# Splitting the last stage's first part into halves, with the last block's squares summed on VectorE and a pile of six blocks

## What is computed

```
def _gn(v, G=16, eps=1e-05):            # mean and variance over H, W and pairs of channels
    g = v.reshape(B_, H_, W_, G, C_ // G)
    return ((g - m) / jnp.sqrt(s + eps)).reshape(v.shape)

def _L3_conv_ref(x, weight, idx_a, idx_b):
    cross = x[..., idx_a] * x[..., idx_b]          # all 496 pairs of a row
    feat = jnp.concatenate([x, x * x, cross], axis=-1)
    return jnp.einsum('bcij,cijo->bcio', feat, weight)

x = x + _L3_conv_ref(_gn(x), ...)
```

## Time and profile before

| | us |
|---|---|
| median of 3 runs | 809.18 |
| lowest and highest run | 802.34, 817.39 |
| the profiled execution | 816.41 |
| its span in the profile | 814.5 |
| the seam's first small reduction to the first gather | 507.10 to 526.56 |

### The profile page before, as it was taken

One profiled execution on the slowest core, in us unless ns is written; L12 is line 12 of the kernel. 1 busy time (PEld: TensorE's weight loads), 2 busy tenths in 40 slices (PEclk: granted clock), 3 DMA queues, 4 the chain that ended last, 5 costly groups with the idle time before them and its releaser, 6 DMA issues.

```text
span 814.5 us, 57339 instructions
## 1 busy us (share of the span) xinstructions
PE 522.6 (64%) x26570; PEld 402.6 (49%) x26570; DVE 576.1 (71%) x698; ACT 435.8 (54%) x724; POOL 294.2 (36%) x412
## 2 busy tenths in 40 slices
PE   0036665326699999437665257167887868878786
PEld 0025555326588878236655222045655546555554
DVE  4989999899543432699989896446765747767563
ACT  5229999491121221359999362235655645656452
POOL 1049884000555520089882021431414224141110
PEclk9996999858799999857889569589998989999897
DMA  8809999400399999439999200458999899999990
GB/s 342 369 11 349 397 397 399 178 0 1 125 319 347 403 402 405 191 109 391 395 397 362 76 1 0 124 157 306 306 380 348 275 332 314 383 357 325 344 340 24
DMA packets 49846, 217.56 MB, mean 267 GB/s; under 512 B 7552, under 2 KB 17792, under 8 KB 29312
## 3 DMA queue, kind: packets, MB, share of 16 engines
q1 hardware_dynamic: 40336, 210.06, 69.7%
q10 hardware_dynamic: 9216, 6.30, 2.5%
q0 software_dynamic: 240, 0.53, 0.2%
HBM read 202.18 MB, written 8.39 MB: 259 GB/s over the span
## 4 chain that ended last, share of the span: by engine, by line
PE 31%; DVE 27%; DMA 17%; issue 9%; POOL 9%; ACT 5%; ACTq 1%; SPq 0%; DVEq 0%; POOLq 0%
PE psum L836 12%; DMA wring<-in_own 9%; DVE stats L631 5%; PE psum L946 5%; PE psum L919 5%; POOL xn_ring L254 4%; PE psum L930 4%; DVE abs_sums L699 3%; DMA wring<-in_w 3%; DMA beyond<-state_b 2%; ACT state_b L598 2%; DVE state_b L799 2%; DVE xn_ring L254 2%; POOL state_a L374 2%; POOL near L385 2%
## 5 line engine op out<-in xcount | busy, mean ns | idle before, releaser
L799 DVE TENSOR_TENSOR state_b<-psum,state_b 128x512 f32<-128x512 f32 x256 | 164.9, 685 | 110.2 <-ACT state_b L598 109.9
L598 ACT ACTIVATE state_b<-psum 128x512 f32<-128x512 f32 x256 | 140.6, 594 | 118.0 <-PE psum L919 114.6
L836 PE MATMUL psum<-signs,near 64*32 64x96 f16 (+3 forms) x6528 | 128.2, 220 | 98.7 <-DMA beyond<-nothing 36.8
L836 PEld LDWEIGHTS psum<-signs,near 64*32 64x32 f16 (+1 forms) x6528 | 115.1, 104 | 107.7 <-issue 107.2
L699 DVE TENSOR_REDUCE abs_sums<-wring 128x1 f32<-128x2048 f32 x64 | 142.9, 2276 | 0.1
L474 ACT ACTIVATE signs<-wring 128x2304 f16<-128x2304 f32 x64 | 134.8, 2107 | 0.0
L946 PE MATMUL psum<-state_b,wring 128*32 128x32 f32 x8192 | 109.5, 204 | 29.0 <-issue 12.0
L946 PEld LDWEIGHTS psum<-state_b,wring 128*32 128x32 f32 x8192 | 90.6, 116 | 67.8 <-issue 30.5
L919 PE MATMUL psum<-signs,sel 64*128 64x512 f16 x512 | 90.9, 409 | 44.4 <-POOL signs L408 19.6
L836 PE MATMUL psum<-wring,near 64*32 64x96 f32 (+5 forms) x3264 | 96.5, 241 | 16.4 <-DMA beyond<-nothing 10.6
L836 PEld LDWEIGHTS psum<-wring,near 64*32 64x32 f32 (+1 forms) x3264 | 86.9, 108 | 23.9 <-issue 23.9
(11 more groups left out here) (141 smaller groups left out, 797.6 us busy)
## 6 DMA issues: line engine op xcount, KB each, us to landing
wring<-in_w SPq DMA_DIRECT2D x96, 1152.0 KB, 10.2
wring<-in_pairs SPq DMA_DIRECT2D x64, 1024.0 KB, 9.2
wring<-in_own SPq DMA_DIRECT2D x32, 256.0 KB, 9.3
wring<-split SPq DMA_DIRECT2D x32, 256.0 KB, 5.3
state_a<-in_x SPq DMA_DIRECT2D x8, 512.0 KB, 9.3
split<-signs SPq DMA_DIRECT2D x8, 512.0 KB, 8.0
out<-state_a SPq DMA_DIRECT2D x32, 128.0 KB, 9.0
beyond<-state_b ACTq DMA_DIRECT2D x112, 32.0 KB, 5.9
```

Of the source, the lines that this page charges most:

```text
L598: act.activation(left[:, n % LSLOTS, :], psum[:, n % ASLOTS, :], ACT.Copy, scale=1.0 / HALF_SCALE / HALF_SCALE).then_inc(left_made, 1)
L799: dve.tensor_tensor(feats[:, n % FSLOTS, :], psum[:, ASLOTS + n % BSLOTS, :], left[:, n % LSLOTS, :], ALU.mult).then_inc(feats_made, 1)
L836: last = pe.matmul(psum[g * B:(g + 1) * B, bank, (a * C) % 512:(a * C) % 512 + (b - a) * C], acts[q, j, s, k, :], weights[q, j, kind, s, ( ...
```

## The change

Three edits. First, the statistics: the pile has six blocks (GpSimd makes five additions) and TensorE takes it right after the sums of block 6; block 7's squares are reduced by VectorE to 32 columns, and TensorE passes these 32 columns through the same matrix into bank 6; VectorE adds the two 32-column results. Second, part 0 is normalised, split into high and low, written to DRAM and read back in two halves of 512 columns, each with semaphores of its own; the first ring copies wait for the first half only. SyncE's queue holds put and get of the first half, put and get of the second, then those of part 1. Third, GpSimd starts part 1 only when the low half of all of part 0 is made.

```diff
--- before.py
+++ after.py
@@ -62,7 +62,8 @@
 FSLOTS = 8
 LSLOTS = 3
 TILES = NK * PT
-PILED = 5
+PILED = 6
+PHALF = PART // 2
 
 
 def build(nc, x, w_conv, bias, gamma_beta, w_pairs, w_own, mats, sel_rows, sel_index, split, out):
@@ -174,11 +175,16 @@
         root = sem("root")
         dve_chain = sem("dve_chain")
         transposed = sem("transposed")
+        half_made = sem("half_made")
+        hi_half = sem("hi_half")
+        lo_half = sem("lo_half")
         part_made = sem("part_made")
         part_centred = sem("part_centred")
         hi_split = sem("hi_split")
         lo_split = sem("lo_split")
         squared = sem("squared")
+        half_out = sem("half_out")
+        half_in = sem("half_in")
         split_out = sems("split_out", V)
         parts_in = sems("parts_in", V)
         ring_made = sem("ring_made")
@@ -322,9 +328,21 @@
                         sp.dma_start(parts[first:first + W, i % 2, :, :],
                                      split[i, k].rearrange("(g w) n -> w g n", g=G)).then_inc(parts_in[i], 16)
 
-            for i in range(2):
-                put_split(i)
-                get_parts(i)
+            for half in range(2):
+                cols = slice(half * PHALF, (half + 1) * PHALF)
+                sp.wait_ge((hi_half, hi_split)[half], 1)
+                sp.wait_ge((lo_half, lo_split)[half], 1)
+                sp.dma_start(split[0][:, :, cols].rearrange("k p n -> p k n"), hi_lo[:, 0, :, cols]
+                             ).then_inc((half_out, split_out[0])[half], 16)
+                sp.wait_ge((half_out, split_out[0])[half], 16)
+                for side in range(2):
+                    for k in range(2):
+                        first = (2 * side + k) * W
+                        sp.dma_start(parts[first:first + W, 0, :, cols],
+                                     split[0, k][:, cols].rearrange("(g w) n -> w g n", g=G)
+                                     ).then_inc((half_in, parts_in[0])[half], 16)
+            put_split(1)
+            get_parts(1)
             for k in range(NK):
 
                 sp.wait_ge(mixed, PT * (k + 1))
@@ -402,7 +420,9 @@
             def copy_ring(k):
 
                 if k % (2 * GROUP) == 0:
-                    pool.wait_ge(parts_in[k // GROUP // 2], 16 * 2 * 2)
+                    pool.wait_ge(parts_in[k // GROUP // 2] if k else half_in, 16 * 2 * 2)
+                if k == GROUP:
+                    pool.wait_ge(parts_in[0], 16 * 2 * 2)
                 if k >= GROUP:
                     pool.wait_ge(gathered, (k - GROUP + 1) * PT)
                 pool.tensor_copy(ring[:, k % GROUP, :].rearrange("p (g n) -> p g n", g=G),
@@ -436,6 +456,7 @@
                 pool.tensor_tensor(dst, dst, r_op, ALU.mult).then_inc(part_made, 1)
 
             pool.wait_ge(part_made, 1)
+            pool.wait_ge(lo_split, 1)
             normalise_part(1)
             for grp in range(NGROUP):
                 copy_ring(grp * GROUP)
@@ -583,7 +604,10 @@
                 act.activation(own_xsq, xn[:, grp // 2 % 2, grp % 2 * GCOLS:(grp % 2 + 1) * GCOLS],
                                ACT.Square).then_inc(squared, 1)
 
-            high(0)
+            act.wait_ge(half_made, 1)
+            act.activation(hi_lo[:, 0, 0, 0:PHALF], xn[:, 0, 0:PHALF], ACT.Copy, scale=HALF_SCALE).then_inc(hi_half, 1)
+            act.wait_ge(part_made, 1)
+            act.activation(hi_lo[:, 0, 0, PHALF:PART], xn[:, 0, PHALF:PART], ACT.Copy, scale=HALF_SCALE).then_inc(hi_split, 1)
             square_own(0)
             high(1)
             for n in range(TILES):
@@ -760,18 +784,32 @@
                                       blk(state_b, m).rearrange("p (w b) -> p b w", b=B)).then_inc(transposed, 1)
 
 
+            dve.wait_ge(squares[3], V)
+            dve.tensor_reduce(red[:, 1, 0:B], blk(state_b, V - 1).rearrange("p (c b) -> p b c", b=B), X, ALU.add
+                              ).then_inc(gn_red[3], 1)
             for side in range(2):
                 dve.wait_ge(gn_acc[3] if side == 0 else gn_sums[3], 1)
                 link(dve.tensor_reduce(red[:, side, 0:B], psum[:, 4 + side, :].rearrange("p (c b) -> p b c", b=B), X, ALU.add))
+            link(dve.tensor_tensor(red[:, 1, 0:B], red[:, 1, 0:B], psum[:, 6, 0:B], ALU.add))
             mn, rs, ta, tb = (t[:, 0:B] for t in (mean, rstd, tmp_a, tmp_b))
             link(dve.tensor_scalar(mn, red[:, 0, 0:B], 1.0 / GN_COUNT, None, ALU.mult))
             link(dve.tensor_tensor(ta, mn, mn, ALU.mult))
             link(dve.scalar_tensor_tensor(tb, red[:, 1, 0:B], 1.0 / GN_COUNT, ta, ALU.mult, ALU.subtract))
             inverse_root(rs, tb, ta, GN_EPS, 6)
-            m_op, r_op = (t.unsqueeze(1).to_broadcast([P, C, B]) for t in (mn, rs))
-            first, old = (t.rearrange("p (c b) -> p c b", b=B) for t in (xn[:, 0, :], state_a[:, 0:PART]))
-            link(dve.tensor_tensor(first, old, m_op, ALU.subtract))
-            dve.tensor_tensor(first, first, r_op, ALU.mult).then_inc(part_made, 1)
+            m_op, r_op = (t.unsqueeze(1).to_broadcast([P, C // 2, B]) for t in (mn, rs))
+            for half in range(2):
+                cols = slice(half * PHALF, (half + 1) * PHALF)
+                first, old = (t[:, cols].rearrange("p (c b) -> p c b", b=B) for t in (xn[:, 0, :], state_a[:, 0:PART]))
+                link(dve.tensor_tensor(first, old, m_op, ALU.subtract))
+                dve.tensor_tensor(first, first, r_op, ALU.mult).then_inc((half_made, part_made)[half], 1)
+
+            def low_half_of(half):
+
+                cols = slice(half * PHALF, (half + 1) * PHALF)
+                dve.wait_ge((half_made, part_made)[half], 1)
+                dve.wait_ge((hi_half, hi_split)[half], 1)
+                dve.scalar_tensor_tensor(hi_lo[:, 0, 1, cols], xn[:, 0, cols], HALF_SCALE, hi_lo[:, 0, 0, cols],
+                                         ALU.mult, ALU.subtract).then_inc((lo_half, lo_split)[half], 1)
 
             def low(i):
                 dve.wait_ge(part_made, i + 1)
@@ -785,7 +823,8 @@
                 dve.tensor_tensor(state_a[:, cols], psum[:, 6 + half % 2, 0:HALF * C4 * B], state_a[:, cols], ALU.add
                                   ).then_inc(result_made, 1)
 
-            low(0)
+            low_half_of(0)
+            low_half_of(1)
             low(1)
             for n in range(TILES):
                 grp, t = n // GT, n % GT
@@ -890,7 +929,7 @@
 
                 for h in range(2):
                     last = pe.matmul(psum[:, 5, :], same_pair, state_b[:, (2 * i + h) * 512:(2 * i + h + 1) * 512],
-                                     start=(i == PILED and h == 0), stop=(i == 0 and h == 1))
+                                     start=(i == 0 and h == 0), stop=(i == V - 2 and h == 1))
                 return last
 
             for i in range(V):
@@ -900,13 +939,14 @@
                                      start=(i == 0 and h == 0), stop=(i == V - 1 and h == 1))
                 if i == V - 1:
                     last.then_inc(gn_acc[3], 1)
+                if i == PILED:
+                    pe.wait_ge(piled, PILED - 1)
+                    squares_of(0)
                 if i > PILED:
                     pe.wait_ge(squares[3], i)
                     squares_of(i - 1)
-            pe.wait_ge(squares[3], V)
-            squares_of(V - 1)
-            pe.wait_ge(piled, PILED - 1)
-            squares_of(0).then_inc(gn_sums[3], 1)
+            pe.wait_ge(gn_red[3], 1)
+            pe.matmul(psum[:, 6, 0:B], same_pair, red[:, 1, 0:B], start=True, stop=True).then_inc(gn_sums[3], 1)
             pe.wait_ge(sel_made, 1)
 
             def gather(j, t):
```

## The result

| | before | changed |
|---|---|---|
| median of 22 runs, us | 809.52 | 805.23 |
| lowest and highest, us | 802.13, 817.39 | 795.66, 813.71 |
| the profiled execution, us | 816.41 | 813.71 |
| its span, us | 814.5 | 811.8 |
| square of block 7 to first gather, us | 26.89 | 17.74 |

The ratio of the times is 0.9926, with a 95% interval from 0.9898 to 0.9954: a gain of 6.0 us, with 3.7 to 8.3 as its interval. (Ratio and interval leave out the runs that took over 1.5% more than the fastest run of the same kernel, seven of the changed kernel and three of the one before.) Over all 22 runs of each kernel the means differ by 4.8 us, with 2.3 to 7.3 as the interval, so the gain is known only to some 2.5 us either way. The profiled execution of the changed kernel was the slowest of its 22. The forecast was 801.5, 7.7 us less.

The account below looks back on a forecast made before the run. It took the last stage to run on its stream of weights, started by the load for k=4. Terms 2.9 + 2.4 + 0.5 + 1.9 = 7.7 us, taken off the median 809.18, gave 801.5; range 792 to 811.

Parts of the forecast that it names:

- Part 1: Statistics at the seam: fewer TensorE passes behind block 7's square, so the first subtraction comes 2.9 us earlier.
- Part 2: First subtraction to first put: halved VectorE and ScalarE operations take 3.65 us instead of 6.06, so -2.4 us.
- Part 3: Trip to DRAM and back by halves: put to get -0.5 us, get to landing 4.7 us, so -1.9.
- Part 4: Work moved behind: ring copies covered by 1.5 us, first eviction and product by 1.1; k=4 load on time or 0.2 late.
- that rival: SyncE late: each half trip costs what a whole one did, delaying the weight stream; 804.5 us, chance 0.15.
- What bounds the kernel: Opening step: no engine alone sets the time; the last stage runs on its weight stream, started by the k=4 load.
- Theory two: Written for the experiments: the last stage gives some gain back, its weight stream being full; the change is worth 6 us.
- Theory one: Written for the experiments: each microsecond at the seam is one at the end; worth 9.1 us, or 8.2 from own terms.
- TensorE's instruction waits: Rival at the last stage's start: holes with no releaser grow beside the half transfers, up to 823 us; chance 0.05.
- The clock: Clock in TensorE's gap at the seam: it falls and returns as before and gives nothing.
- Dear halves: Rival at the seam: VectorE's halves not sped up and 1 KB packets dear; gain 4.3 to 5.3, 804 us, chance 0.10.

Follow-up runs that it names:

- the late stream: Changed kernel with SyncE's loads for k=4 and k=5 held until k=2 is mixed; ratio 0.9938 to the kernel before.
- the delayed changed kernel: Changed kernel with 13 chained VectorE operations on scratch before the first subtraction; ratio 1.0000 to the kernel before.
- relieved pair: Kernel before and changed kernel, each with pair weights of k=4 to 63 loaded by half; medians 784.47 and 779.51 us.
- cut pair: Kernel before and changed kernel, each with the last stage cut to its first 16 of 64 steps k; medians 609.75 and 601.96 us.

## Why the prediction was right, and where it was not

The direction, the class and the range held. The parts, by the prediction's own steps:

| step | forecast, us | measured, us |
|---|---|---|
| part 1, statistics | -2.9 | -3.2 |
| part 2, to the first put | -2.4 | -2.6 |
| part 3, put to get | -0.5 | -0.65 |
| part 3, get to first gather | -1.9 | -2.7 |
| seam to the first gather | -7.7 | -9.15 |
| first gather to own terms | not priced | +0.9 |
| seam to the own terms | -7.7 | -8.2 |
| time | -7.7 | -6.0 (-8.3 to -3.7); means of all runs -4.8 (-7.3 to -2.3) |

**Part 1** held. The matmul of 32 columns took 0.30 (taken 0.4). The pile was ready 1.6 us before its slot, as worked out. Block 7's reduction took 1.95 (taken 1.88) and ended under TensorE's passes.

**Part 2** held, with VectorE's halves at 0.69 and 0.68. It was 0.2 quicker, because two operations that don't wait for each other overlap a little: the second subtraction starts at 509.41, 0.08 before the first product ends, where I had put a gap of 0.03 after it.

**Part 3** has the term that was mis-sized most. I took 4.7 from the get's issue to its landing. GpSimd's copy starts 4.02 after that issue. Two stretches of the half get, and behind them two of the whole get before:

```profile
513.65:514.60 0.95, 0.00 (x0) 0.00 (x0) 0.00 (x0) 0.00 (x0) 0.95 (x1) 0.50 0.00 0
514.60:517.70 3.10, 0.00 (x0) 0.00 (x0) 0.00 (x0) 0.49 (x1) 2.52 (x3) 0.50 0.80 254
```

```profile
519.11:520.00 0.89, 0.00 (x0) 0.00 (x0) 0.38 (x1) 0.41 (x1) 0.00 (x0) 0.50 0.00 0
520.00:525.75 5.75, 0.00 (x0) 0.00 (x0) 0.84 (x1) 0.00 (x0) 0.00 (x0) 0.50 0.97 244
```

In both cases no byte moves for the first 0.9 us. Then the engines move 244 GB/s in the one and 254 in the other, and what they move is more than the get: the next put is issued 1.86 us after the first get and goes beside it, 0.35 MB of it in the second stretch before and all 0.26 MB after. My reading of 243 GB/s at full share took that put's bytes, and a first microsecond without any, for the get alone. It left 4.3 of the 6.64 to be halved and 2.33 to stay. The rows say 5.75 to be halved and 0.9 to stay: 0.9 + 2.9 = 3.8, against the 4.02 measured. So the fixed part was taken too large. Whether packets of 1 KB cost more or less by the byte than those of 2 KB these rows don't separate; the two rates differ by 4%. The Trainium skill's 2.0 us for each transfer ("DMA: Bandwidth & Descriptors", section "Anatomy of one DMA") gave 2.6 for the half put; it took 2.16 to the next issue. Here the row and half its bytes were nearer.

**Part 4.** The covers of the ring copies and of the first eviction held. The cover of the first product was 1.1 us by my sum and was used up, since the first gather came 1.4 earlier against the square than I had it: VectorE's low part of part 1 ended at 519.9, as forecast by that count, and the first product began 1.40 after the first gather instead of 1.27. TensorE then waited 1.2 us at 520.71 for GpSimd's own copy, which the low part had stretched from 0.61 to 1.61. I had priced neither this copy nor the collision; it is the 0.9 that the gain loses by the own terms. It did not move the load for k=4, which came 8.87 after the first gather. My sentence that holding GpSimd back "costs cover and no time" came out right at the own terms (20.98 and 21.06 without it), but for a reason that it didn't have: the collision only changes its place. SyncE was free at 526.5, 0.8 before the load for k=4 was wanted, as worked out; so that rival did not come, and by the late stream it would have cost little if it had: a load 14 us later cost 1 us by the middle values.

**What bounds the kernel** failed as a step. I read the DMA share of 0.99 as proof that the last stage "runs on its stream of weights". The late stream and the halved weights show TensorE's start and its 259 us to be the base, with the stream as an addition. The forecast survived this by luck, because TensorE's start and the stream's moved by nearly the same amount.

**The sum against the time.** The seam gained 9.15 at the first gather and the time 6.0. That the forecast of 7.7 lies near the measured time is in part two errors of opposite sign. The four terms of the seam together were sized 1.45 too low, over half of it (0.8) the get. Against that stand 0.9 lost at the own copy and some 2 us that never arrived, 3 or more by the means of all runs. Theory two, that the full stage gives them back, is not supported: delays come through whole, the delayed changed kernel is at 1.0000, and the relieved stage, where nothing waits for weights, keeps 8.5 of 9.1 and still shows only 3.4 to 7.8 in the times. Theory one isn't confirmed either. Counted to the first gather, 9.1 us would be 0.9888, just outside the interval of the changed kernel; counted to the own terms, 8.2 us would be 0.9899, just inside it, but outside the 2.3 to 7.3 of all runs. In the relieved pair's two profiled executions (span 785.3 and 779.1) the seam is 9.1 shorter, the stage is equal, and the 3.0 that are missing lie ahead of block 7's square (499.55 and 502.51). In the cut pair this stretch was 2.8 shorter in the changed kernel instead (500.18 and 497.38). Of the change only the pile's fifth addition and the pile's passes lie in this stretch, and they make the last step between two squares 3.35 to 3.48 us in the nine kernels that have them, against 3.21 to 3.27 in the other five, so 0.1 us more. Over all kernels it lies between 497.4 and 502.5. Its mean is 499.5 in the four kernels that have neither edit and 499.5 in the eight that have both, with some 1.5 us of uncertainty, so the traces give no sign that the new program makes the first three layers longer. Where the rest went stays open; what is shown is that 0.9 of the 9.15 is lost before the own terms and that the stage's rest doesn't take it.

The load for k=4 to the end of the span took 284.5 us instead of 279.1, where I had written that 2 us either way for a reason of the change would prove me wrong. The scatter of 17 us between stages of the same code leaves that sign undecided; the relieved pair, with 258.8 in both, speaks for no change.

**The other rivals.** TensorE's instruction waits did shift, but didn't grow. In the first 16 us behind the first gather the longest wait with no releaser is 1.7 to 2.6 us in the five kernels without halves and 2.4 to 3.3 in the seven with halves cut in the middle. Over the first 40 us all such waits add up to 7.1 us on average in either group, and from first gather to end the cut pair has 82.4 and 82.7. My price for the case in which they grow was wrong besides: 29 us of waits on top of 801.5 are 830, not 823. The clock was at 0.50 when TensorE began again, before and after. Dear halves did not come.

## What to carry to other kernels

Between two stages, while the busiest engine is idle, each step can be priced from the trace to a few tenths of a microsecond, and cutting the first piece of work small shortens each link of the chain behind it. Measure the gain again a few instructions into the next stage: here 9.15 us at the first gather were 8.2 three microseconds later, because the earlier start brought two engines to collide. Take a transfer's fixed part from the stretch in which no byte moves, and look what else is in flight before you halve the rest. A DMA share near 1 does not say how much of a stage is the DMA's: delay the first load, or halve the bytes, and see. When a trace's stage times scatter by 17 us, judge an edit of 9 us by the short stretch that it changes and by many timed runs, never by the difference of two spans.

## What the runs showed of the hardware

- A GpSimd copy of 128x512 took 0.61 us alone and 1.61 beside a VectorE operation on two SBUF inputs; a VectorE low half took 0.69 alone and 2.59 beside GpSimd's subtraction. Side by side the pairs took 2.03 and 3.28 us, one after the other they would take 1.83 and 3.03: nothing was won by the overlap.
- A get of four transfers moved no byte for 0.9 us after its first issue, whole (0.89) or halved (0.95). Together with the put beside it, it then ran at 244 GB/s with 1.05 MB to get and at 254 with 0.52 MB.
- Loads issued 14 us late into a stage with four filled slots cost about 1 us by the middle values (up to 5 are possible), in a stage whose DMA share is near 1 afterwards.
